# An audio layer on one core: the router's first layer in another PSUM bank, and two rounding steps in another order

## The reference, cut to what matters

```python
xf = x.reshape(b * n, d)
logits = _gelu(xf @ router_w1 + router_b1) @ router_w2 + router_b2
probs = jax.nn.softmax(logits, axis=-1)
topk_p, topk_i = jax.lax.top_k(probs, K)           # 2 of 8 experts
...
for _ in range(ITERS):                             # 2 iterations
    ctx = jnp.concatenate([integrated, v], axis=-1)
    shared_ctrl = _gelu(ctx @ shared_w1 + shared_b1) @ shared_w2 + shared_b2
    ...
    ctrl = _experts(ctx_e, flat_idx, expert_w1, expert_b1, expert_w2, expert_b2)
    ...
refined = _gelu(integrated @ refine_w1 + refine_b1) @ refine_w2 + refine_b2
out = xf + integration_weight * refined
```

## Time and profile before

| | us |
|---|---|
| median of 3 runs | 765.87 (765.49 to 766.56) |
| profiled execution | 766.59 |
| span of its trace | 764.8 |
| TensorE busy | 724.5 (95%) |
| VectorE busy | 626.5 (82%) |
| ScalarE busy | 598.1 (78%) |
| GpSimd busy | 377.8 (49%) |

### The profile page before, as it was taken

How to read it: one execution, slowest core, us unless ns; L and a number is a source line. 1 busy time by engine, 2 the same in 40 slices (tenths; PEclk the granted TensorE clock), 3 DMA queues, 4 the chain that set the end, 5 groups by cost and what they waited for, 6 DMA issues and landing times.

```text
span 764.8 us, 14327 instructions
## 1 busy us (share of the span) xinstructions
PE 724.5 (95%) x4516; PEld 615.4 (80%) x4516; DVE 626.5 (82%) x1430; ACT 598.1 (78%) x1382; POOL 377.8 (49%) x438
## 2 busy tenths in 40 slices
PE   5667999999999999999999999999999999999976
PEld 3446788888888888888888888887988888887876
DVE  3857788988988988988988988988889889888762
ACT  4765778788788788888888878888888888776672
POOL 1426456555555555555645545555555564563210
PEclk9888999999999999999999999999999999999995
DMA  8300000000000000000000000000000000000000
GB/s 330 124 15 1 8 1 17 6 22 8 15 22 1 21 21 3 20 23 1 22 22 1 22 21 1 21 22 1 21 21 1 8 8 2 8 9 1 8 8 14
DMA packets 11611, 17.27 MB, mean 23 GB/s; under 512 B 1232, under 2 KB 10504, under 8 KB 11024
## 3 DMA queue, kind: packets, MB, share of 16 engines
q1 hardware_dynamic: 11536, 16.35, 6.3%
HBM read 13.20 MB, written 3.15 MB: 21 GB/s over the span
## 4 chain that ended last, share of the span: by engine, by line
PE 89%; DVE 4%; ACT 3%; issue 2%; POOL 1%; DMA 1%; SPq 0%; ACTq 0%; POOLq 0%; DVEq 0%
PE ctl L495 23%; PE ctl L511 11%; PE ctl L472 5%; PE ctl L501 4%; PE ctl L514 4%; PE cd L593 4%; PE pa L593 4%; PE cd L472 3%; PE cd L666 3%; PE ctl L562 3%; PE ctl L481 2%; PE pa L588 2%; PE cd L588 2%; PE pb L593 2%; PE ctl L482 2%
## 5 line engine op out<-in xcount | busy, mean ns | idle before, releaser
L375 POOL TENSOR_TENSOR hm_lo<-gl,mexp 128x256 fp32r<-128x256 f32 x144 | 128.1, 914 | 100.0 <-DVE gl L1257 96.5
L495 PE MATMUL ctl<-w2e_hi,hm_hi 128*128 128x512 f32 (+1 forms) x432 | 158.6, 376 | 0.1
L495 PE MATMUL ctl<-w2e_lo,hm_hi 128*128 128x512 f32 (+1 forms) x432 | 150.8, 362 | 0.0
L495 PEld LDWEIGHTS ctl<-w2e_hi,hm_hi 128*128 128x128 f32 x432 | 82.2, 190 | 22.2 <-DVE hm_hi L1243 7.9
L511 PE MATMUL ctl<-w2e_hi,hm_lo 128*128 128x512 f32 (+1 forms) x432 | 99.9, 357 | 0.0
L1243 DVE TENSOR_TENSOR hm_hi<-ge,mexp 128x256 fp32r<-128x256 f32 x144 | 89.2, 634 | 12.4 <-ACT ge L946 9.4
L965 ACT ACTIVATE work<-ctl 128x256 f32<-128x256 f32 (+1 forms) x144 | 69.6, 484 | 35.4 <-PE ctl L514 27.4
L495 PEld LDWEIGHTS ctl<-w2e_lo,hm_hi 128*128 128x128 f32 x432 | 82.4, 191 | 10.6
L511 PEld LDWEIGHTS ctl<-w2e_hi,hm_lo 128*128 128x128 f32 x432 | 74.6, 188 | 13.7 <-POOL hm_lo L375 0.3
L381 POOL TENSOR_TENSOR rg_lo<-rg,rg_hi 128x512 fp32r<-128x512 f32 x23 | 33.2, 1445 | 74.9 <-ACT rg_hi L902 74.8
L917 ACT ACT_TABLE_LOAD x49 | 62.9, 1283 | 0.9
(11 more groups left out here) (210 smaller groups left out, 2061.4 us busy)
## 6 DMA issues: line engine op xcount, KB each, us to landing
work<-params_dram SPq DMA_DIRECT2D x3, 1152.0 KB, 12.6
xT<-turned_dram SPq DMA_DIRECT2D x24, 128.0 KB, 2.2
out_dram<-y SPq DMA_DIRECT2D x24, 128.0 KB, 1.7
xa<-x_dram SPq DMA_DIRECT2D x16, 128.0 KB, 2.3
par<-params_dram SPq DMA_DIRECT2D x1, 1280.0 KB, 10.3
work<-params_dram SPq DMA_DIRECT2D x2, 512.0 KB, 10.9
xa<-x_dram SPq DMA_DIRECT2D x8, 119.0 KB
par<-params_dram SPq DMA_DIRECT2D x1, 512.0 KB, 15.7
```

The source lines that it names most:

```text
L375: TT(hm[1][:, j, c, :], gl[:, c, part, :], pairs(tile, j, c), ALU.mult).then_inc(done, 1)
L495: mm(dst[:, a:z], hm[0][:, j, c, :], w2e[i][:, c, a:z], start=(c == 0 and i == 0), stop=False)
```

## The change

The router's first layer goes to the free quarter of `pb` (columns 384 to 511) instead of `pd`. TensorE waits for the rounded copy of xf ahead of the router's second layer, which still goes to `pd`, and no longer ahead of the first. Ahead of the first it waits, beside the plain copy, for the reads of `pb` that came before: the halt values of tiles t and m, and the shared units of the tile before f. gelu of the router reads `pb`. On ScalarE the rounding of the refine units is a function of its own, `refine_rounded`, and is done between the plain and the rounded copy of xf; in rounds without a tile f it stays behind the gelus, and the newest tile keeps its own order.

```diff
@@ TensorE
                 if f.exists():
                     passed(pe, xfT_sb, f)
-                    passed(pe, xfh_sb, f)
+                    if t.exists():
+                        passed(pe, th1_sb, t)
+                    if m.exists():
+                        passed(pe, th2_sb, m)
+                    passed(pe, s1_sb, f, back=1)
                     if f.low == 0:
                         pe.wait_ge(par_in[1], 16)
-                    hidden(pd, HID, w1r, range(1), xfT, KD, rh_ps)
+                    hidden(pb[:, 3 * P:4 * P], HID, w1r, range(1), xfT, KD, rh_ps)
...
                 if f.exists():
                     passed(pe, rh_sb, f)
+                    passed(pe, xfh_sb, f)
                     mm(pd[:, 0:E], rh[:, :], pv("w2r", HID), start=True, stop=True).then_inc(lg_ps, 1)
@@ ScalarE
                 if not o.newest():
                     last.then_inc(rg_sb, 1)
-                    passed(act, rg_sb, o)
-                    passed(act, rl2_ps, o, back=1)
-                    AF(rgp[0][:, :, :], rg[:, :, :], ACT.Copy).then_inc(rgh_sb, 1)
+
+            def refine_rounded(o):
+
+                passed(act, rg_sb, o)
+                passed(act, rl2_ps, o, back=1)
+                AF(rgp[0][:, :, :], rg[:, :, :], ACT.Copy).then_inc(rgh_sb, 1)
...
                     refine_units(o)
+                    if not f.exists() and not o.newest():
+                        refine_rounded(o)
 
                 if f.exists():
                     passed(act, e_ps, f, back=1, per=2)
                     passed(act, rh_ps, f, back=1)
                     passed(act, xfl_g, f, back=1)
                     state(xfT, pd, D, f, xfT_ps, xfT_sb)
+                    if o.exists():
+                        refine_rounded(o)
                     state_hi(1, pd, f, xfh_sb, f)
                     passed(act, rh_ps, f)
-                    AF(rh[:, :], pd[0:HID, 0:P], ACT.Gelu, bias=pv("b1r", HID)).then_inc(rh_sb, 1)
+                    AF(rh[:, :], pb[0:HID, 3 * P:4 * P], ACT.Gelu, bias=pv("b1r", HID)).then_inc(rh_sb, 1)
```

## The result

The changed kernel took 764.6 us (median of 14 runs, 762.36 to 765.31) against 765.99 (14 runs, 764.34 to 767.16) for the one before: ratio 0.9978, 95% interval 0.9969 to 0.9988. That is 0.22% faster, with 0.12% to 0.31% in the interval. The same program beside other runs of the kernel before (e4) gave 0.9992, which is not told from no change. The profiled execution took 763.86 us, its span 762.1.

The account below looks back on a forecast made before the run. TensorE, busy 95% of the span and all of a steady round, was taken as the bound; -0.8 us in 19 rounds and -0.2 in the first made -1.0, from 765.87 to a median of 764.9 us, range 763.3 to 766.8.

Parts of the forecast that it names:

- The sum: Whole kernel: -0.8 us from 19 rounds at 0.04 and -0.2 from the first round, giving -1.0 us.
- the 0.39: TensorE, L514 start to router's first layer: 0.04 us is the rounded copy's wait, 0.33 the weight-tile change, which stays.
- one early round: TensorE round without refine units: nothing holds the router's layer, yet it starts 0.33 us after L514.
- the 0.14 us: Rounded copy's end to router's layer start; also used in the first round, 0.37 - 0.14 = 0.23 us can go.
- The added waits: TensorE's waits for earlier pb reads ahead of the router's first layer: cost 0, at most 0.05 us a round.
- The new order: ScalarE, refine rounding after the plain copy: costs nothing under the 0.80 us idle; without that cover, 0.28 us a round.
- the hole: ScalarE, before the plain copy of xf where the refine rounding was: some 0.3 us, taken from idle time.
- the slower rival: GpSimd's low part of x1 starts late, delaying the picking chain 0.2 us a round: 768.7 us, chance 0.12.
- The cover: GpSimd, between the end of the moved low part of xf and the start of x1's: 0.31 us.
- The first rival: TensorE, L514 to router's layer: more than the wait goes, 0.10 us a round, giving 763.8 us; chance 0.10.
- The third: TensorE's sequencer: added waits take the 0.04 us that the old one gave back, 766.1 us; chance 0.10.
- The step that failed: TensorE, busy all 29.14 us of a steady round: a wait on any other engine is worth nothing by itself.

Follow-up runs that it names:

- e4: The changed kernel again, same program, beside other runs of the kernel before: 763.94 us against 764.45, ratio 0.9992.
- e1: Kernel before plus only the new place of the router's sums (pb), ScalarE's order kept: 764.48 us against 764.45, ratio 0.9997.
- e6: Kernel before with only its two waits ahead of the router's first layer in reversed order: 764.97 us against 765.13, ratio 0.9998.
- e5: Changed kernel with the router's two layers on 128 x 128 weight tiles: 762.14 us, ratio 0.9963 to the kernel before.
- e7: Kernel before with one more, long-over wait paired with that for the rounded copy, sums still in pd: ratio 0.9984 to the kernel before.
- e2: Kernel before with only ScalarE's new order, the router's sums still in pd: 772.44 us, ratio 1.0099.
- e8: Changed kernel with the refine units' rounding moved behind the rounded copy of xf: ratio 0.9993 to the kernel before.
- e10: Changed kernel with VectorE's low part of the shared units moved between the two additions of summed: 760.26 us, ratio 0.9944 to the kernel before.
- e9: The kernel with 128 x 128 router tiles, plus VectorE's shared low part between the two additions of summed: 754.69 us against 764.69 for the kernel before.

## Why the prediction was right, and where it was not

**The size.** The sum was -1.0 us: 0.8 in the rounds and 0.2 in the first. The traces have 0.85 over 18 rounds (of which one, with the router's layer at 534 us, was 0.05 longer before) and 0.10 of the first round by the second picking. The measured ratio gives 1.7 us (0.9 to 2.4). The repeat on another occasion, e4, gives 0.6 (-0.4 to 1.5), and e1 and e6, whose rounds are those of the changed kernel, 0.2 both. I take it that the effect is near the 1.0 of the traces and that the first comparison got some of its 1.7 from the clock at the end of the runs, as the two profiled executions did; how the runs themselves were divided is not shown, so the last 0.7 us stay open.

**The wait and what stays of the 0.39.** Right: 0.042 us a round against 0.04, and 0.32 left against 0.33. That the rest is the change of tile size was argued from one early round, and it was too much: e5 shows that 0.09 of the 0.32 goes with the smaller tile. The other 0.23 is there with a 128 x 128 tile as well; the neighbouring matmuls of L511, also with 512 columns, follow each other at about the same 0.23. The Trainium skill's rule that a change of tiling mode drains TensorE (TensorEngine Tiling (Array Packing), "Key Properties") agrees, and the number here is 0.319 - 0.233 = 0.09 us for this change.

**What kind of wait it was.** Here the prediction was right for a reason that was only half right. I took the 0.14 us from the end of the copy to the matmul as the copy's, and its removal as the only way to the gain. e6 and e7 show that this distance hangs on the form of the wait: in the medians 0.14 alone, 0.10 in a pair, and 0.07 on the weight load, where it holds nothing, with the copy in the same place and the sums in the same bank. The change gained by not having this one wait late. The same 0.14 was wrong in the first round, where the sum let 0.23 of the 0.37 us go: the released wait rides on the weight load, the layer starts 0.04 after the copy, and 0.33 went (0.29 by the first picking).

**The added waits.** Right: no cost. The distance with all of them is 0.319, that of e6 with none of them.

**The new order.** Right: the hole was 0.31 (0.3 predicted), the idle time before gelu 0.48 (0.45). e1 shows that it gives nothing, e2 what it would cost without the cover: 0.29 us a round, where I had 0.28.

**GpSimd and the slower rival.** The cover was 0.44 us, not 0.31, because the low part of the refine units shrank to 1.27 us. It no longer starts under VectorE's long gate instruction (L1315, which ended at 388.19 before); that this is the reason was not tested by itself. The scan ended with GpSimd's instruction as before (0.66 us). The rival needed 1.76 us; e8 used up another 0.28 of the cover and still lost at most 0.02 a round. It is ruled out. The prediction's argument that an instruction with one SBUF tensor input is not held did not bear out, though: in e8 one was, by 0.05 us (L1408). Its other argument carried the forecast, that the scan would end with GpSimd's instruction in any case.

**The first rival** (more than the wait goes) is ruled out by the distance of 0.319. **The third** (the added waits take the gain back) by the same.

**The step that failed** is in the first part: "a wait on any other engine is worth nothing by itself", read from a TensorE that is busy for all of 29.14 us. Rows of matmuls overlap in the profile and their ends are modelled, so such a wait lies under the end of the row before it. The changed kernel is busy 29.10 of 29.10 us too:

```profile
384.00:413.10 29.10, 29.10 (x190) 24.93 (x189) 25.33 (x59) 24.38 (x58) 15.66 (x19) 1.00 0.04 14
```

and 0.15 of them hung on VectorE, as e10 shows. It did no harm to the forecast, because VectorE's chain starts from the router's second layer and moved with it. But it would have sent a reader away from a place worth more than three times as much as this change.

## What to carry to other kernels

A busy TensorE is not a TensorE that never waits: look at the starts of its matmuls and compare each step with the same step where nothing holds it, in an early round or in a variant. Where a wait comes late on TensorE, try which of its waits rides on the weight load before changing where data lies. A saving at one place is worth its size only up to the slack of the next chain; here 0.29 us of tile changes gave 0.10 until VectorE's instruction was moved.

## What was not expected of the hardware

- How long a late wait holds TensorE depends on its form: alone in its instruction it ended 0.079 us after the semaphore's update, in a pair 0.034, on the weight load 0.042 (medians of the traces).
- From a 128 x 128 float32 weight tile to one of the faster format with 512 columns to multiply the starts lay 0.031 us apart when nothing waited (e10, e9).
- VectorE's scan over eight columns took 0.174 us in the first two rounds, where no GpSimd instruction runs beside it, and 0.65 to 0.67 in all others of the changed kernel, always ending 0.03 after GpSimd's; it took 0.76 in e5 and 0.62 in e8, where it started at another distance from that instruction. The Trainium skill's rule of the exclusive port pair (SBUF — State Buffer, "SBUF: two separate sides") agrees. In e8, of the instructions with one SBUF tensor input, the addition that reads PSUM and the search for the highest values took 0.17 us under a GpSimd instruction as without, but the comparison with a scalar (L1408) took 0.28 instead of 0.23 and ended with GpSimd's.
